# A fused LayerNorm, random-feature and feed-forward kernel: rows turned by VectorE through DRAM, plain float32 dot products, GpSimd's queue rearranged

## The reference

```python
def _rfs(xw, ab, AB, gs):
    dot_products = jnp.einsum('...d,rd->...r', xw, ab[:, None] * gs)
    correction = (0.5 * jnp.sum(xw * xw, axis=-1))[..., None] * (ab * ab)
    return 1.0 / math.sqrt(NUM_RFS) * AB * jnp.exp(dot_products - correction)

xn = _layernorm(x)
s = jnp.einsum('bsr,or->bso', _rfs(xn, ...), _rfs(input_weights, ...))   # 256 features, 256 outputs
h = silu(xn @ w1.T * w1_s) * (xn @ w2.T * w2_s)          # 256 -> 1024
h = gelu(h @ h1.T * h1_s)                                # 1024 -> 1024
h = gelu(h @ h2.T * h2_s)                                # 1024 -> 1024
x = x + s * silu(h @ w3.T * w3_s)                        # 1024 -> 256
```

## Time and profile before

| | |
|---|---|
| median of 3 runs | 1330.39 us (1328.18 to 1330.98) |
| the profiled execution | 1328.22 us, its span in the trace 1326.4 us |
| TensorE matmuls | 1303.6 us busy, 98% of the span, 6300 instructions |
| VectorE | 944.5 us, 71% |
| ScalarE | 754.2 us, 57% |
| GpSimd | 598.7 us, 45% |
| DMA | 194.93 MB, 147 GB/s on the mean |
| granted TensorE clock | 0.998 of full speed |

### The profile page before, as it was taken

The page is one execution under the profiler, slowest core; times in us unless marked ns, Lnnn a source line. Parts: engine busy times, 40 slices in busy tenths (PEclk is TensorE's granted clock), DMA queues, the critical chain, the costliest instruction groups (busy, mean ns, idle before and its releaser), DMA issues.

```text
span 1326.4 us, 16508 instructions
## 1 busy us (share of the span) xinstructions
PE 1303.6 (98%) x6300; PEld 1103.4 (83%) x6300; DVE 944.5 (71%) x1205; ACT 754.2 (57%) x1016; POOL 598.7 (45%) x618
## 2 busy tenths in 40 slices
PE   7988999999999999999999999999999999999998
PEld 6877898888988888888888888888898888988887
DVE  7696867778677886688875776656767567665665
ACT  5455655566546664466654666546565465655664
POOL 5883978898788996889877000000000000000000
PEclk9999999999999999999999999999999999999999
DMA  9998841554625444255443444334442344514441
GB/s 240 327 331 254 275 116 57 194 169 157 112 91 180 155 147 128 93 174 163 134 120 111 145 141 99 108 113 142 153 103 78 127 153 133 128 48 135 135 159 50
DMA packets 98692, 194.93 MB, mean 147 GB/s; under 512 B 19120, under 2 KB 21424, under 8 KB 97584
## 3 DMA queue, kind: packets, MB, share of 16 engines
q1 hardware_dynamic: 85648, 156.06, 37.7%
q0 software_dynamic: 12960, 37.76, 9.9%
HBM read 168.58 MB, written 31.49 MB: 151 GB/s over the span
## 4 chain that ended last, share of the span: by engine, by line
PE 88%; DMA 5%; DVE 3%; POOL 2%; ACT 1%; issue 1%; SPq 0%; POOLq 0%; DVEq 0%
PE ps L216 68%; PE ps L219 19%; DVE quad L199 2%; DMA ring<-in_h 1%; DMA s<-in_h 1%; DMA q_h<-sm 1%; DVE split L199 1%; DMA hs<-quad 1%; PE ps L303 1%; DMA w<-in_w 1%; DMA ry<-in_x 1%; POOL ry L505 1%; POOL quad L505 0%; POOL s L505 0%; DVE xin L205 0%
## 5 line engine op out<-in xcount | busy, mean ns | idle before, releaser
L216 PE MATMUL ps<-split,ring 128*128 128x512 f32 x2800 | 765.3, 390 | 7.9 <-DMA ring<-in_h 4.4
L216 PEld LDWEIGHTS ps<-split,ring 128*128 128x128 f32 x2800 | 526.3, 188 | 118.3 <-issue 4.8
L199 DVE TENSOR_TENSOR split<-quad,split 128x1024 fp32r<-128x1024 f32 x258 | 339.6, 1324 | 189.6 <-ACT split L195 189.0
L195 ACT ACTIVATE split<-quad 128x1024 fp32r<-128x1024 f32 x258 | 267.1, 1052 | 71.8 <-PE ps L219 71.8
L219 PE MATMUL ps<-split,ring 128*128 128x512 f32 x784 | 305.0, 389 | 0.0
L216 PE MATMUL ps<-xT,w 128*128 128x512 f32 x768 | 216.3, 390 | 1.0 <-DVE ry L199 0.9
L549 POOL TENSOR_TENSOR cube<-cube,seen 128x256 f32<-128x256 f32 x176 | 200.1, 1137 | 14.3
L195 ACT ACTIVATE quad<-ps 128x512 f32<-128x512 f32 x192 | 114.6, 598 | 131.0 <-PE ps L219 129.9
L195 ACT ACTIVATE quad<-quad,cols 128x512 f32<-128x512 f32 (+1 forms) x194 | 139.1, 719 | 86.3 <-DVE quad L199 84.8
L199 DVE TENSOR_TENSOR quad<-quad 128x1024 f32<-128x1024 f32 x128 | 177.2, 1425 | 5.8 <-DMA hs<-quad 5.8
L219 PEld LDWEIGHTS ps<-split,ring 128*128 128x128 f32 x784 | 147.3, 188 | 30.6
(11 more groups left out here) (92 smaller groups left out, 1026.3 us busy)
## 6 DMA issues: line engine op xcount, KB each, us to landing
ring<-hs SPq DMA_DIRECT2D x428, 256.0 KB, 3.6
xin<-in_x SPq DMA_DIRECT2D x17, 512.0 KB, 5.5
s_h<-s SPq DMA_DIRECT2D x16, 512.0 KB, 2.9
seen<-in_h POOLq DMA_DIRECT2D x64, 128.0 KB, 3.4
ry<-in_x SPq DMA_DIRECT2D x15, 512.0 KB, 5.6
out<-ry SPq DMA_DIRECT2D x15, 512.0 KB, 2.6
ring<-in_h POOLq DMA_DIRECT2D x20, 256.0 KB, 12.8
hs<-in_h SPq DMA_DIRECT2D x5, 1024.0 KB, 7.8
```

Of the source, the lines that this page charges most:

```text
L195: return act.mark(lambda e: e.activation(dst, src, func, scale=scale))
L199: return dve.mark(lambda e: e.tensor_tensor(dst, a, b, op))
L216: pe.run(lambda e: e.matmul(dst, stat, mov, start=start, stop=stop, skip_group_check=loose))
```

## The change

For the tiles from 1 on:

- The TensorE transposes go. `rows_out` stores the normalised rows of a half from `xin` to a DRAM tensor `z_h` on GpSimd's queue, in four transfers of 1024 runs of 128 bytes, so that 32x32 blocks lie in the order of the transposed half; `rows_in` loads them into the low slot of `xT`; `turn_blocks` transposes within the 32x32 blocks by two VectorE instructions into `xTf`, which is the buffer of `xin`, and ScalarE casts the high part; `split_rows` subtracts the low part.
- h0's rows go out at L0 (5,3), h1's at L1 (0,3). At L1 (1,3) GpSimd issues the stores of the norms of both halves, the loads of both halves' blocks, the broadcasts of the norms, and then counts 16 chunks, instead of all 88 in one go. The turning stands at L1 (5,2) and (6,2), the subtracts at (5,3) and (6,3).
- The normalises and the other small tasks move ahead to L0 (2,2) to L1 (1,3); the loads of the next tile's rows move from L0 (0,3) to (1,0).

For all tiles the dot products are plain float32: two matmuls of 128x512 for each r on `xTf`, and `PT` has one part. In the first tile `turn_rows` stays, with a VectorE copy to `xTf` added; GpSimd's copy of block A22 of the second layer goes to SyncE, at L1 (0,2), and its load of w3 to the start of L1.

```diff
-            PT = sf("PT", [P, 2, KD, R], F32R)
+            PT = sf("PT", [P, KD, R])
...
+        z_h = nc.dram_tensor("z_h", [2, 4, 32, NB * KD, 4, 32], F32).ap()
...
                     def one(e, b=b, kd=kd):
                         return e.transpose(ps[:, banks[kd], b * P:(b + 1) * P], xin[j][:, b, kd * P:(kd + 1) * P], ident[:, :])
                     turned[kd] = pe.mark(one) if b == NB - 1 else pe.run(one)
-            tok = turned[-1]
             for kd in range(KD):
                 hi = cast(xT[j][:, kd, 0, :], ps[:, banks[kd], :], turned[kd], *xT_free.get(h - 2, []))
                 xT_lo[h] = vv(xT[j][:, kd, 1, :], ps[:, banks[kd], :], xT[j][:, kd, 0, :].bitcast(F32), ALU.subtract, hi)
-                free[banks[kd]] = [xT_lo[h]]
-            xin_free[j] = [tok]
+            for kd in range(KD):
+                xTf_done[h] = vcopy(xTf[j][:, kd, :], ps[:, banks[kd], :], turned[-1])
+                free[banks[kd]] = [xTf_done[h]]
+        def rows_out(h):
+            j = h % 2
+            pool.wait(xn_done[h, NB - 1], *([d_zin[j].token] if h - 2 in z_stored else []))
+            for c in range(4):
+                z_stored[h] = d_zout[j].send(pool, z_h[j][:, :, :, c, :].rearrange("a i n j -> i n a j"),
+                                             xin[j][32 * c:32 * c + 32, :, :].rearrange("i b (k a j) -> i (b k) a j", k=KD, a=4))
+        def rows_in(h):
+            j = h % 2
+            pool.wait(z_stored[h], *xT_free[h - 2])
+            d_zin[j].send(pool, xT[j][:, :, 1, :].bitcast(F32), z_h[j].rearrange("a i n c j -> (a i) (n c j)").rearrange("p (c t) -> p c t", c=2))
+        def turn_blocks(h):
+            j = h % 2
+            dve.wait(d_zin[j].token)
+            for kd in range(KD):
+                src = xT[j][:, :, 1, :].bitcast(F32).rearrange("p c (b k n) -> p c b k n", b=2, k=KD)[:, :, :, kd, :]
+                dst = xTf[j][:, kd, :].rearrange("p (c b n) -> p c b n", c=2, b=2)
+                xTf_done[h] = dve.mark(lambda e, dst=dst, src=src: e.transpose(dst, src))
+            xT_hi[h] = cast(xT[j][:, :, 0, :], xTf[j][:, :, :], xTf_done[h], *xT_free[h - 2])
+        def split_rows(h):
+            j = h % 2
+            xT_lo[h] = vv(xT[j][:, :, 1, :], xTf[j][:, :, :], xT[j][:, :, 0, :].bitcast(F32), ALU.subtract, xT_hi[h])
         def norms_out(h):
-            sp.wait(norm_done[h]())
-            q_stored[h % 2] = d_qout[h % 2].send(sp, q_h[h].rearrange("b p -> p b"), sm[:, 3, 4 * (h % 2):4 * (h % 2) + 4], allow_slow_non_contiguous=True)
+            lane, i = (sp, h) if h < 2 else (pool, 2 + h % 2)
+            lane.wait(norm_done[h]())
+            q_stored[h % 2] = d_qout[i].send(lane, q_h[h].rearrange("b p -> p b"), sm[:, 3, 4 * (h % 2):4 * (h % 2) + 4], allow_slow_non_contiguous=True)
         def norms_in(h):
             j = h % 2
-            sp.wait(q_stored[j], *qrow_free[j])
-            qrow_done[h] = d_qin[j].send(sp, qrow[j], q_h[h].rearrange("b p -> (b p)").partition_broadcast(P))
+            lane, i = (sp, h) if h < 2 else (pool, 2 + j)
+            lane.wait(q_stored[j], *qrow_free[j])
+            qrow_done[h] = d_qin[i].send(lane, qrow[j], q_h[h].rearrange("b p -> (b p)").partition_broadcast(P))
         def w12_ready(m):
...
         def dots(h, banks, place):
             j = h % 2
             for r in range(KD):
-                pe.wait(xT_lo[h], *free[banks[r]])
-                tok = group(ps[:, banks[r], :], [(PT[:, wh, kd, r * P:(r + 1) * P], xT[j][:, kd, g, :])
-                                                 for kd in range(KD) for wh in range(2) for g in range(2)])
+                pe.wait(xTf_done[h], *free[banks[r]])
+                tok = group(ps[:, banks[r], :], [(PT[:, kd, r * P:(r + 1) * P], xTf[j][:, kd, :]) for kd in range(KD)])
                 i = at_stage[0] % 2
                 at_stage[0] += 1
                 ex = vst(stage[i][:, :], qrow[j][:, :], ab2[:, r:r + 1], ps[:, banks[r], :], ALU.mult, ALU.add,
...
-            xT_free[h] = [tok]
+            xin_free[j] = [tok]
...
-            copy_raw(pool, 1, ["A22"])
-            d_w3.send(pool, w3[:, :, :], w_kpm["w3"])
-        def count_good():
+        counted_chunks = [0]
+        def count_good(some):
...
             def step(dst, a, b, op):
                 pool.wait(pool.mark(lambda e: e.tensor_tensor(dst, a, b, op)))
-            d_seen[0].send(pool, seen[0][:, :], chunks[0])
-            for n in range(len(chunks)):
+            first = counted_chunks[0]
+            last = counted_chunks[0] = min(first + some, len(chunks))
+            if first == 0:
+                d_seen[0].send(pool, seen[0][:, :], chunks[0])
+            for n in range(first, last):
                 if n + 1 < len(chunks):
                     d_seen[(n + 1) % 2].send(pool, seen[(n + 1) % 2][:, :], chunks[n + 1])
                 v = seen[n % 2][:, :]
...
                 fills.append(count_odd)
-            def norms_away():
-                if t + 1 < NT:
-                    norms_out(h0 + 2)
-                    norms_out(h1 + 2)
+            def later(f, *hs):
+                return [lambda: [f(h) for h in hs]] if t + 1 < NT else []
+            def count_some():
+                if t < FLAG_TILE:
+                    counted[0] = count_good(16)
             sums = [sub(L0, n, g) for n in ("t1", "t2") for g in range(2)]
...
                     load_x(h)
             product_layer(L0, L1, {
-                (0, 0): [] if t else sums[:2], (0, 1): [] if t else sums[2:], (0, 2): [sub(L0, "t3", 0)], (0, 3): [sub(L0, "t3", 1), next_rows],
-                (1, 0): [split(L0, "t2", 0)], (1, 1): [split(L0, "t2", 1)], (1, 2): [sub(L0, "t4", 0)], (1, 3): [sub(L0, "t4", 1)],
+                (0, 0): [] if t else sums[:2], (0, 1): [] if t else sums[2:], (0, 2): [sub(L0, "t3", 0)], (0, 3): [sub(L0, "t3", 1)],
+                (1, 0): [split(L0, "t2", 0), next_rows], (1, 1): [split(L0, "t2", 1)], (1, 2): [sub(L0, "t4", 0)], (1, 3): [sub(L0, "t4", 1)],
                 (2, 0): [split(L0, "t1", 0)], (2, 1): [split(L0, "t1", 1)], (2, 2): [fill, fill], (2, 3): [fill, fill],
                 (3, 0): [split(L0, "t3", 0)], (3, 1): [split(L0, "t3", 1)], (3, 2): [fill, fill], (3, 3): [fill, fill],
-                (4, 0): [split(L0, "b22", 0)], (4, 1): [split(L0, "b22", 1)],
-                (5, 0): [split(L0, "t4", 0)], (5, 1): [split(L0, "t4", 1)], (5, 2): [fill],
+                (4, 0): [split(L0, "b22", 0)], (4, 1): [split(L0, "b22", 1)], (4, 3): [fill],
+                (5, 0): [split(L0, "t4", 0)], (5, 1): [split(L0, "t4", 1)], (5, 2): [fill], (5, 3): [fill] + later(rows_out, h0 + 2),
                 (6, 0): [split(L1, "b11", 0)], (6, 1): [split(L1, "b11", 1)], (6, 2): [sub(L1, "t1", 0)], (6, 3): [sub(L1, "t1", 1)]})
             jobs = {
-                (0, 0): [split(L1, "b21", 0)], (0, 1): [split(L1, "b21", 1)], (0, 2): [sub(L1, "t2", 0)], (0, 3): [sub(L1, "t2", 1)],
+                (0, 0): [split(L1, "b21", 0)], (0, 1): [split(L1, "b21", 1)], (0, 2): [sub(L1, "t2", 0), fill], (0, 3): [sub(L1, "t2", 1), fill] + later(rows_out, h1 + 2),
                 (1, 0): [split(L1, "t2", 0)], (1, 1): [split(L1, "t2", 1)], (1, 2): [sub(L1, "t3", 0)],
+                (1, 3): [fill] + later(norms_out, h0 + 2, h1 + 2) + later(rows_in, h0 + 2, h1 + 2) + later(norms_in, h0 + 2, h1 + 2) + [count_some],
                 (2, 0): [split(L1, "t1", 0)], (2, 1): [split(L1, "t1", 1)], (2, 2): [sub(L1, "t3", 1)], (2, 3): [sub(L1, "t4", 0)],
                 (3, 0): [split(L1, "t3", 0)], (3, 1): [split(L1, "t3", 1)], (3, 2): [sub(L1, "t4", 1)], (3, 3): [split(C, "b11", 0, 2)],
                 (4, 0): [split(L1, "b22", 0)], (4, 1): [split(L1, "b22", 1)], (4, 3): [split(C, "b11", 1, 2)],
-                (5, 0): [split(L1, "t4", 0)], (5, 1): [split(L1, "t4", 1)], (5, 2): [fill, fill], (5, 3): [fill, fill],
-                (6, 0): [split(C, "b22", 0, C.slot)], (6, 1): [split(C, "b22", 1, C.slot)], (6, 2): [fill, fill], (6, 3): [fill, fill, fill, fill, norms_away]}
+                (5, 0): [split(L1, "t4", 0)], (5, 1): [split(L1, "t4", 1)], (5, 2): later(turn_blocks, h0 + 2), (5, 3): later(split_rows, h0 + 2),
+                (6, 0): [split(C, "b22", 0, C.slot)], (6, 1): [split(C, "b22", 1, C.slot)], (6, 2): later(turn_blocks, h1 + 2), (6, 3): later(split_rows, h1 + 2)}
             if t == 0:
-                counted[0] = count_good()
-                for w, (layer, name) in enumerate(((0, "A11"), (0, "A12"), (0, "A22"), (1, "A11"), (1, "A12"))):
+                d_w3.send(pool, w3[:, :, :], w_kpm["w3"])
+                for w, (layer, name) in enumerate(((1, "A22"), (0, "A11"), (0, "A12"), (0, "A22"), (1, "A11"), (1, "A12"))):
                     jobs[w, 2] = jobs.get((w, 2), []) + [lambda layer=layer, name=name: copy_raw(sp, layer, [name])]
             product_layer(L1, C, jobs)
             quad_free[C.at["b22"]] = [C.ready["b22"]]
...
             def between(n):
                 if t == FLAG_TILE and n == 0:
```

(42 more changed lines are left out.)

## The result

The changed kernel takes 1361.5 us (median of 4 runs, 1358.9 to 1363.9) against 1330.7 for the kernel before in the same session: a ratio of 1.0239, 95% interval 1.0214 to 1.0263. It is slower by some 31 us; the forecast was 1351 in a range of 1312 to 1372.

A forecast was written before the change was run, and what follows sets the result against it. TensorE's own instructions bound the steady part. From 1328.2 us: -11.2 transposes, -3.0 dot products, -0.9 ry wait, +1 first tile, +35 q_h stalls give 1349.1; with 2.2 for the median, 1351, range 1312 to 1372.

The forecast's parts named there:

- The wait for ry: TensorE's wait for VectorE's ry, behind the q_h stores on SyncE, goes when both transfers are on GpSimd's queue: 0.9 us gained.
- the cover: Between VectorE's last split before `down` and the matmul needing it: 3.5 us, so the added VectorE work costs nothing.
- rival C: The z_h stores are priced by their number, holding feeds up: 1450 us and more, everything above 1372 counted; chance 0.12.
- The stall behind q_h: q_h stores at (1,3) of the second layer make ring pieces late: 5.0 us per tile, seven tiles, 35 us.
- of 10.0 us from 782.5: Second layer, behind (1,3): the q_h stores' block on other transfers starts at their issue, 782.5, and ends at 792.5.
- The first two will be in: Of four ring pieces under way at the q_h stores' issue, two land in time; the last two are caught.
- The six other tiles show the same pattern: In the kernel before, everything else stood still for 10.0 us behind tile 2's q_h stores, and likewise in other tiles.
- The z_h stores [...] Cost nothing: The 128-byte-run stores take 8 us per half, well inside 49 us, and only share the engines with the ring's loads.
- the sentence on the xT loads in the block: Were all four pieces in, the next feed would land 1 to 3 us late, two 512 KB loads waiting in the block.
- Rival B: The q_h stores' block does not bite, the fourth piece being there by 791.1: about 1316 us (1311 to 1321); chance 0.36.
- The raw feed behind the z_h stores: First tile: the feed waits behind four z_h stores on GpSimd's queue, 5.4 us plus 1.5 for half clock; net +1.
- A: The main sum, with q_h stores stalling TensorE 3 to 7 us per tile: 1351 us (1337 to 1365); chance 0.45.

The follow-up runs named there:

- e2: The changed kernel with neither the z_h stores nor the xT<-z_h loads issued; 1316.5 us, ratio 0.9937 to the kernel before.
- e7: The changed kernel with the z_h stores but without the xT<-z_h loads; 1338.4 us, ratio 1.0076 to the kernel before.
- e8: e1 with q_h in 16-byte pieces for all tiles and the first tile's first z_h stores one step later, at (6,0) of the first layer; 1307.8 us.
- e1: Late norms: the changed kernel with q_h stores back at (6,3) of the second layer and their broadcasts in `down`, both on SyncE's queue; 1310.5 us.
- e3: The changed kernel with q_h laid out by partition, a half's store being 128 pieces of 16 bytes instead of 512 of 4; 1314.6 us.
- e10: e1 with the first tile's first z_h stores at (6,0) of the first layer and q_h in 16-byte pieces for later tiles alone; 1307.9 us.

## Why the prediction was right, and which of its steps was not

**Removed work.** Transposes: 11.2 us forecast, 11.7 measured in `down`. Dot products, from the timeline of TensorE:

```profile
393.31 1.02 PE L218 MATMUL ps<-xin,PT 128*128 128x512 f32 x2
...
400.17 0.59 PE L218 MATMUL ps<-WS,quad 128*128 128x256 f32 x2
```

Four r in 6.86 us, 1.715 each where 1.72 was taken; tile 0's share went into a wait of 0.8 us for WS, so 2.7 and not 3.0. The wait for ry gave 1.2 and not 0.9.

**VectorE and GpSimd.** VectorE's groups by line, and the DMA issues of the whole span:

```profile
L335 DVE STREAM_TRANSPOSE xin<-xT 128x512 f32<-128x512 f32 x28 | 18.1, 684 | 0.0
```

```profile
z_h<-xin POOLq DMA_DIRECT2D x56, 128.0 KB, 3.8
```

684 ns stand against 685 taken, and the cover held: `down` took 15.35 to 15.39 us in six of tiles 0 to 6, and 15.62 in the other. The z_h stores, 128 KB each, land in 3.8 us at the median, a half's four in some 7 us from the first issue (8 taken), so rival C is out: 128-byte runs were not priced like 4-byte ones.

**The stall behind q_h.** 5.0 us per tile forecast, 5.3 measured in tiles 1 to 6: 3.3 idle, where 3.5 was taken (its own landings, 793.5 to 796.5 against 791.1, give 3.9 on the mean), and 1.9 behind it, where 1.5 was taken as lower clock; of the 1.9 the clock is 1.1. The last two pieces are caught, as forecast, in five tiles of these six. But the number was right for a reason that was incomplete. The step that failed reads: the block "of 10.0 us from 782.5". By it all four pieces would have been caught, the first being due at 781.3 + 2.8 = 784.1. "The first two will be in" follows from no row. The block begins later. "The six other tiles show the same pattern" was misread: the trace of before shows it in tile 3, in a DMA window that I had not read closely (654 to 676, slices of 0.55 us; stores issued at 658.34, ring pieces from 659.30 on):

```profile
GB/s 41 0 0 0 0 0 0 60 171 10 4 16 149 216 78 0 0 4 30 30 4 22 11 15 15 11 7 11 7 26 86 179 257 291 402 298 272 298 369 376
```

216 GB/s still flow at 661.4, some 3 us behind the issue; the fall to nothing comes at 662.2, 3.9 us behind it. After the change traffic falls under 100 GB/s 3.8 us behind the issue in tile 2 (472.77 to 476.6), and 3.2 to 5.2 us behind it in tiles 1 to 6. In tiles 1 and 5 of before it looks as in tile 3; in the other four nothing got through behind the issue, so on SyncE's queue the beginning varies. From 782.5 a beginning 3.9 us later is 786.4, when the last piece was due to land (786.2): without other traffic the four pieces are just in, as e2 shows in tiles 2 to 6. What catches the third and the fourth is the step "The z_h stores [...] Cost nothing": their duration was near (7 us for 8), but they slow the feed by about a microsecond at the one place where it has none to spare. In tile 2 the third piece is issued 0.3 us ahead of the q_h stores and the first lands after 3.5 us; in e2 it is 1.05 us and 2.9 us. And the sentence on the xT loads in the block, which I had kept for the case that all four were in, is worth more than half of the loss: without the loads 18 of the 40 us are left (e7). Rival B's condition, that the fourth piece is there in time, was met by the block alone in tiles 2 to 6, and e2's 1316.5 us are B's 1316; I gave it 0.36 for another reason.

**The first tile.** Forecast: +1 net for the raw feed and one stall of 5.0. Measured: +0.8 up to the first layer, for which there was no term, and +13.8 in the layers. The raw feed behind the z_h stores came as forecast in kind, with 2.6 us of waits for 5.4 taken, and a net of -1.1 in place of +1. Mis-sized was the stall: it cost 15.2 us. The waits there were 6.56, 3.20 and 0.60 us, and the granted clock was 0.51 from 145 to 152 us and 0.57 from 158 to 166. Beside the q_h stores the first tile copies 1 MB blocks (`hs<-in_h`) on SyncE's queue; that they lengthen the stall was not tried by itself. With late norms tile 0 takes 109.5. These 10 us are nearly all that the time lies above the forecast of 1351. The range, 1312 to 1372, reached over A and B alike; that the time lies in it says less than the place and the size of the stall.

## What to carry to other kernels

A slow small transfer is judged by where it stands: the same store was free in a stretch that fed on nothing and cost 5 us a tile where a piece of the ring has 8.4 us to land. When a stall hangs on such a margin, add up everything that moves in the window, transfers that are cheap by themselves too; here either z transfer pushed the feed past it. And read when a block begins and ends in a window that has traffic in it, not from the issue of the store.

## What had not been expected of the hardware

- Two stores of 512 pieces of 4 bytes left the queues working for 3.2 to 5.2 us after their issue (tiles 1 to 6 of the changed kernel), then stopped nearly all traffic until they landed; 16-byte pieces in place of 4-byte ones cut the time from issue to landing from 12.2 to 5.5 us.
- In e8's first tile five of VectorE's eleven 128x4 instructions from 18.8 to 30.5 us took 1.14 to 1.32 us, the others 0.15 to 0.16 as nearly all do in e1, while GpSimd was busy 15.4 instead of 12.4 us of the 16 from 14 to 30. A shorter store in the first tile thus made the start 4 us later (63.4 in e8 and 62.9 in e3, 59.6 in e10, which packs the later tiles alone). That GpSimd's additions were the cause was not tried by itself.
